# Another order of the query tiles of a head pair, with the turned probabilities kept in other slots by other engines

## The chip, the cores and the metric

One core of one Trainium2 chip runs the whole kernel. The metric is the device time of one execution in microseconds; the median of three executions of the kernel before is 360.82 us.

## The reference, cut to what matters

A decoder layer on x of shape 2 x 512 x 128, in fp32: causal self-attention, a differential cross-attention over a context of 154 rows, and a quantised feed-forward block with a convolution. The change touches the self-attention alone:

```python
q = einsum('ntc,hdc->nhtd', layernorm(x), w_q)        # 16 heads of 64; k and v likewise
a = einsum('nhtd,nhsd->nhts', q, k) / 8
a = where(causal_forbidden, -inf, a)                   # key s > query t is cut
a = softmax(a, axis=3)
y = einsum('nhts,nhsd->nthd', a, v).reshape(n, t, -1) @ w_o
x = x + y
```

## The kernel before

The 16 heads of 2 batch rows are worked off as 16 steps n (`STEPS`), each one pair of heads a = 0, 1 of one batch row. The 512 queries of a pair are four query tiles t = 0 to 3 of 128. Because of the causal mask tile t needs only its first 128(t+1) keys, so tiles 3, 2, 1, 0 are 512, 384, 256 and 128 wide. `ROUNDS` (line 39) packs them in three rounds r: tile 3, tiles 2 and 0 side by side in a bank of 512, tile 1. Round k = 3n + r uses one of two pairs of PSUM banks in turn (`SP[k % 2]`).

A round passes through all engines. TensorE writes the scores (`scores`, matmuls on `qs`, then four small mask matmuls that put -1e30 on what the mask cuts). VectorE takes the row maxima (`row_max`, lines 1122 and 1128). ScalarE takes the exponentials with the row sums (`exps`, line 414; each is followed by a short read of the accumulator). VectorE inverts the sums (`invert_sums`, line 1136) and GpSimd multiplies by them (`normalise`, line 299). TensorE turns the probabilities (`turn`, line 677) in transposes of 64 columns: 16 for a round of 512, 8 for tile 1. Rounds 0 and 1 are turned into the banks PT and PT+1, round 2 into PJ0 and OB. The turned blocks are copied from PSUM to slots of `pT` in SBUF: round 0 half by VectorE (`keep_turned`, line 1150) and half by ScalarE (`keep_half`, line 423), round 1 by VectorE, round 2 by ScalarE (`keep_short`, line 435). Slots 0 and 3 alternate from step to step for tile 3. When all three rounds of a pair are there, TensorE multiplies them with v (`weighted`, ten matmuls per head pair, bank OB), and ScalarE copies the result to `onT` (`copy_heads`, line 445).

Every engine has one queue in order, written out by hand. In step n TensorE does: scores(n,0), turn(n-1,1), scores(n,1), turn(n-1,2), scores(n,2), project(n+1) for keys (bank PJ0) and queries (bank PT), weighted(n-1), turn(n,0). VectorE does: keep_turned(n-1,0), row_max(n,0), keep_turned(n-1,1), invert_sums(n,0), row_max(n,1), row_max(n,2), keys(n+1), invert_sums(n,1), invert_sums(n,2). ScalarE does: copy_heads(n-2), keep_half(n-1), exps(n,0), keep_short(n-1), exps(n,1), query(n+1), exps(n,2). GpSimd normalises rounds 0, 1, 2. Some steps have more behind them: quantise_weights on VectorE after steps 2 and 3, the output projection of the first batch row in step 9, a layer norm on VectorE and ScalarE after step 10 and on VectorE after step 11.

The waits that matter here stand in `scores` and `turn`: scores of round k may start once the exponentials of round k-2 have read their banks, and turn(n,1) may start once the copies of turn(n,0) have emptied the banks PT and PT+1:

```python
if k >= 2:
    pe.wait_ge(exp_done, EXPS[k - 1])     # in scores(n, r), k = 3n + r
...
if r == 1:
    pe.wait_ge(pt_dve, 2 * n + 1)         # in turn(n, r)
    pe.wait_ge(pt_act, 2 * n + 1)
```

After the last step the cross-attention begins: query_parts(0) on ScalarE (its turn stands between exps(15,1) and exps(15,2)), query_rows(0) on VectorE after the last invert_sums, then cross_max(0,0) on TensorE, between whose rounds the last turns and the last weighted sum are placed.

Of the kernel before, what the change touches and what calls it, by code (L numbers as in the profile page):

```python
# [8 lines left out]
ALU = mybir.AluOpType  # L9
# [3 lines left out]
P = 128  # L13
# [25 lines left out]
ROUNDS = [[3], [2, 0], [1]]  # L39
# [18 lines left out]
for _k in range(48):  # L58
    MAXES.append(MAXES[-1] + (2 if _k % 3 == 0 else 1))


PLACE = ({3: 0, 2: 1, 1: 2, 0: 3}, {2: 0, 1: 1, 3: 2, 0: 3})


def decoder_layer(nc, x, consts, wqk, wv, wo, ctxT, xwq, xbq, xwk, xbk, xwv, xbv, xwo, xbo, lam_in,
                  w1, cw, cb, w2, out):
    with ExitStack() as ctx:
# [100 lines left out]
        prob = (pT[:, 4, :, :], pr[:, 0:2, :], pr[:, 2, :].rearrange("p (a n) -> p a n", a=2))  # L168
# [98 lines left out]
        def _(pool):  # L267
# [24 lines left out]
            def normalise(n, r):  # L292
                pool.wait_ge(inv_done, 3 * n + r + 1)
                at = 0
                for t in ROUNDS[r]:
# [70 lines left out]
        def _(act):  # L366
# [38 lines left out]
            def exps(n, r):  # L405
# [4 lines left out]
                for t in ROUNDS[r]:  # L410
                    w = P * (t + 1)
                    for a in range(2):
                        act.wait_ge(max_done, MAXES[k] + 1 + a if r == 0 else MAXES[k + 1])
                        nc.scalar.activation(prob[r][:, a, at:at + w], bank[:, SP[k % 2] + a, at:at + w], ACT.Exp,  # L414
                                             bias=nmax[:, t, a:a + 1], accum_out=psum[:, t, a:a + 1]).then_inc(exp_done, 1)
                    at += w

            def keep_half(n):

                act.wait_ge(t_ps, 3 * n + 1)  # L420
                if n >= 2:
                    act.wait_ge(u_ps, n - 1)
                nc.scalar.copy(turned_to(3 * (n % 2), 2 * NT)[:, 1], turned_from(PT, PT + 2, 2 * NT)[:, 1]).then_inc(
                    pt_act, 1)

            def keep_short(n):

                act.wait_ge(t_ps, 3 * n + 3)
                if n >= 1:
                    act.wait_ge(u_ps, n)  # L430
                for half, at in enumerate((PJ0, OB)):
                    whole = pT[:, 2, :, :]
                    dst = bass.AP(whole.tensor, whole.offset + 64 * half,
                                  [list(whole.ap[0]), [T, 2], [P, 2], [1, 64]])
                    last = nc.scalar.copy(dst, bank[:, at, 0:2 * P].rearrange("p (a i q) -> p a i q", a=2, i=2))
                last.then_inc(pt_act, 1)
# [51 lines left out]
            for n in range(1, STEPS):  # L488
                if n >= 2:
                    copy_heads(n - 2)  # L490
                keep_half(n - 1)
                exps(n, 0)
                keep_short(n - 1)
                exps(n, 1)
                if n + 1 < STEPS:
# [5 lines left out]
                exps(n, 2)  # L501
# [3 lines left out]
            keep_half(STEPS - 1)  # L505
            keep_short(STEPS - 1)
# [95 lines left out]
        def _(pe):  # L602
# [8 lines left out]
            def project(n, w):  # L611
# [7 lines left out]
                if n >= 2 and w == 1:  # L619
                    pe.wait_ge(pt_act, 2 * n - 2)  # L620
# [28 lines left out]
            def turn(n, r):  # L649

                k, blocks = 3 * n + r, (NT, NT, 2)[r]
# [5 lines left out]
                if r == 1:  # L657
                    pe.wait_ge(pt_dve, 2 * n + 1)
                    pe.wait_ge(pt_act, 2 * n + 1)
# [21 lines left out]
            def weighted(n):  # L681

                b, p, odd = n // NPAIR, n % NPAIR, n % 2
                pe.wait_ge(pt_dve, 2 * n + 2)
                pe.wait_ge(pt_act, 2 * n + 2)
                three = slice(odd, odd + 3)
                two = slice(1, 4, 2) if odd else slice(0, 2)
                one = 3 if odd else 0
                for j in range(NT):
                    for a in range(2):  # L690
                        own = slice(DH * a, DH * a + DH)
                        o = bank[own, OB, :].rearrange("p (t q) -> p t q", q=P)
                        v = v_sb[:, b, j, 2 * p + a, :]
                        keys = slice(P * j, P * j + P)
                        if j == 0:
                            mm(o[:, 0:3, :], v, pT[:, three, a, keys], True, False, skip_group_check=True)
                            mm(o[:, 3, :], v, pT[:, 1, a, 3 * P:4 * P], False, False, skip_group_check=True)
                        elif j == 1:
                            mm(o[:, 0:3, :], v, pT[:, three, a, keys], False, False, skip_group_check=True)
                        elif j == 2:  # L700
# [803 lines left out]
```

## Time and profile before

| | |
|---|---|
| median of 3 executions | 360.82 us (359.97 to 361.19) |
| profiled execution, its own time | 358.9 us |
| span of the profiled execution | 356.7 us |
| TensorE busy | 307.7 us, 86% |
| VectorE / ScalarE / GpSimd busy | 226.1 / 212.4 / 121.3 us |
| self-attention, start to last step | about 14 to 198 us of the span |
| mean granted TensorE clock | 0.964 |

Between the first and the last instruction lie 356.7 us; 2.2 us of the profiled execution lie around them. A timeline row has start, duration, engine, line, operation, and in brackets how long the engine idled before it and on whom it waited. PE is TensorE, PEld its weight loads, DVE VectorE, ACT ScalarE, POOL GpSimd.

### The profile page before, as it was taken

The numbers are of one execution on the slowest core, as the hardware profiler recorded it, in microseconds if no ns is written. First come the engines' busy times: TensorE is split into PE (matmuls) and PEld (weight loads), VectorE is DVE, ScalarE is ACT, GpSimd is POOL, SyncE is SP. The second block draws the span as 40 slices with busy tenths as digits, with TensorE's granted clock in tenths as the row PEclk, the third lists the DMA queues.
The fourth block names the chain that finished last, engine by engine and source line by source line (L and its number), as shares of the span: only waits on it lengthen the run. The fifth ranks groups of instructions, "written<-read, shape, count | busy, mean of one in ns | idle before, by whom it ended". The sixth has DMA issues, their size and how long they took to land.

```text
span 356.7 us, 6631 instructions
## 1 busy us (share of the span) xinstructions
PE 307.7 (86%) x2454; PEld 202.4 (57%) x2454; DVE 226.1 (63%) x507; ACT 212.4 (60%) x520; POOL 121.3 (34%) x193
## 2 busy tenths in 40 slices
PE   1797899989999998889997799969999897988795
PEld 0564665666666775656664467735655562465463
DVE  3854667776666527676666564576777768068554
ACT  3465577767777618867774173576786368436154
POOL 4623547774477646625642020113330000000000
PEclk9999899999999999999996889999999999999696
DMA  7800000000000000000000000000000000000001
GB/s 286 299 1 2 0 3 1 2 2 2 3 0 3 2 2 1 2 2 0 2 3 3 0 0 2 0 0 3 0 1 2 0 3 0 0 0 2 0 23 38
DMA packets 4834, 6.17 MB, mean 17 GB/s; under 512 B 833, under 2 KB 3649, under 8 KB 4674
## 3 DMA queue, kind: packets, MB, share of 16 engines
q1 hardware_dynamic: 4514, 5.42, 4.3%
q8 instruction: 19, 0.31, 0.4%
q10 hardware_dynamic: 288, 0.33, 0.3%
q14 instruction: 13, 0.11, 0.1%
HBM read 5.23 MB, written 0.52 MB: 16 GB/s over the span
## 4 chain that ended last, share of the span: by engine, by line
PE 57%; DVE 20%; ACT 14%; issue 6%; POOL 1%; DMA 1%; ACTq 0%; DVEq 0%
PE bank L604 51%; ACT pr L414 4%; ACT pT L414 3%; DVE nmax L1122 3%; DVE nmax L1128 3%; PE bank L677 2%; DVE pT L1150 2%; ACT pT L520 2%; PE bank L805 1%; DVE qk L1179 1%; DVE xn L1072 1%; ACT v_sb L525 1%; DVE onT L1302 1%; DVE stats L1059 1%; POOL pr L299 1%
## 5 line engine op out<-in xcount | busy, mean ns | idle before, releaser
L1179 DVE TENSOR_REDUCE qk<-bank 128x4 fp32r<-128x616 f32 x64 | 49.2, 797 | 24.6 <-PE bank L604 24.3
L520 ACT ACTIVATE pT<-bank 128x512 f32<-128x512 f32 (+1 forms) x80 | 45.0, 600 | 28.4 <-PE bank L604 27.3
L299 POOL TENSOR_SCALAR pr<-pr,pinv 128x384 f32<-128x384 f32 (+2 forms) x96 | 46.3, 505 | 45.1 <-DVE pinv L1136 45.1
L414 ACT ACTIVATE pr<-bank,nmax 128x384 f32<-128x384 f32 (+2 forms) x96 | 44.7, 482 | 18.2 <-DVE nmax L1128 18.2
L604 PE MATMUL bank<-qs 64*128 64x512 f32 (+3 forms) x256 | 49.0, 464 | 4.6 <-ACT pT L414 4.6
L604 PE MATMUL bank<-pT,v_sb 128*64 128x128 f32 (+2 forms) x320 | 39.5, 394 | 0.0
L309 POOL TENSOR_TENSOR km<-kb_,con 128x1232 fp32r<-128x1232 f32 x8 | 18.0, 2248 | 59.4 <-PE bank L604 57.4
L604 PE MATMUL bank<-km,qk 128*128 128x308 f32 x128 | 33.7, 347 | 3.9 <-ACT pr L414 2.0
L1150 DVE COPY pT<-bank 128x512 f32<-128x512 f32 (+1 forms) x32 | 30.4, 951 | 6.8 <-PE bank L677 6.7
L414 ACT ACTIVATE pT<-bank,nmax 128x512 f32<-128x512 f32 x32 | 21.7, 683 | 20.4 <-DVE nmax L1122 20.4
L604 PEld LDWEIGHTS bank<-pT,v_sb 128*64 128x64 f32 x320 | 21.8, 140 | 19.1 <-issue 16.9
L604 PEld LDWEIGHTS bank<-km,qk 128*128 128x128 f32 x128 | 23.8, 197 | 13.5 <-DVE qk L1179 5.0
L604 PE MATMUL bank<-qk,km 128*128 128x512 f32 x64 | 28.5, 451 | 2.3 <-ACT pT L520 2.0
L1128 DVE TENSOR_REDUCE nmax<-bank 128x2 f32<-128x768 f32 (+2 forms) x48 | 29.9, 676 | 0.6 <-PE bank L604 0.6
L299 POOL TENSOR_SCALAR pT<-pT,pinv 128x512 f32<-128x512 f32 x32 | 21.9, 697 | 21.4 <-DVE pinv L1136 21.4
L1136 DVE RECIPROCAL pinv<-psum 128x2 f32<-128x2 f32 x64 | 8.5, 157 | 29.0 <-ACT pr L414 28.1
L604 PEld LDWEIGHTS bank<-qs 64*128 64x128 f32 x256 | 20.2, 188 | 7.5 <-ACT pT L414 6.2
L1122 DVE TENSOR_REDUCE nmax<-bank 128x1 f32<-128x512 f32 x32 | 20.6, 683 | 4.2 <-PE bank L604 4.2
L604 PEld LDWEIGHTS bank<-mask_b,sel_b 64*128 64x128 bf16 x256 | 13.9, 94 | 16.3 <-issue 12.3
L677 PE MATMUL bank<-con,pr 64*128 64x64 f32 x384 | 18.4, 227 | 4.6 <-POOL pr L299 3.0
L414 ACT ACTIVATION_READ_ACCUMULATOR pr<-bank,nmax 128x1 f32 x96 | 20.5, 213 | 0.0
L604 PE MATMUL bank<-qk,wqk_h 128*128 128x512 f32 x48 | 19.2, 444 | 1.4 <-DVE wqk_l L1367 1.4
(162 smaller groups left out, 596.8 us busy)
## 6 DMA issues: line engine op xcount, KB each, us to landing
pT<-in_wqk SPq DMA_DIRECT2D x1, 1024.0 KB, 6.0
cw_sb<-in_cw SPq DMA_DIRECT2D x1, 768.0 KB, 8.9
x_sb<-in_x SPq DMA_DIRECT2D x2, 256.0 KB, 5.2
pT<-in_wv SPq DMA_DIRECT2D x1, 512.0 KB, 6.7
wo_sb<-in_wo SPq DMA_DIRECT2D x1, 512.0 KB, 7.2
out<-x_sb SPq DMA_DIRECT2D x8, 64.0 KB, 1.5
onT<-in_consts ACTq DMA_DIRECT2D x1, 256.0 KB, 6.5
pT<-in_xwk SPq DMA_DIRECT2D x1, 256.0 KB, 7.2
```

Source lines behind the costliest of these rows:

```text
L299: nc.gpsimd.tensor_scalar(d, d, pinv[:, t, a:a + 1], 1.0, ALU.mult, ALU.mult).then_inc(norm_done, 1)
L309: nc.gpsimd.tensor_tensor(km[:, g, :, :], _repeat(kb_[:, g, b, :], GP), _bcast(con[:, C_ROWM:C_ROWM + GP], S2), ALU.mult).then_inc(km_done, 1)
L414: nc.scalar.activation(prob[r][:, a, at:at + w], bank[:, SP[k % 2] + a, at:at + w], ACT.Exp, bias=nmax[:, t, a:a + 1], accum_out=psum[:, t ...
L520: nc.scalar.activation(px[rows, v % 10, :], bank[rows, (ST0, ST1)[v % 2], :], ACT.Exp, scale=SD ** -0.5).then_inc(xexp_done, 1)
L525: nc.scalar.copy(ut[:, G // NG, 2 * (G % NG) + u, :], bank[:, OB, :]).then_inc(ut_done, 1)
L604: return nc.tensor.matmul(out_, lhsT, rhs, start=start, stop=stop, **kw)
L677: last = nc.tensor.transpose(bank[:, to, at:at + 64], prob[r][own, a, P * i:P * i + P], con[own, C_ID + 64 * half:C_ID + 64 * half + 64])
L1122: nc.vector.tensor_reduce(nmax[:, NT - 1, a:a + 1], bank[:, SP[k % 2] + a, :], AX.X, ALU.max, negate=True).then_inc(max_done, 1)
L1128: last = nc.vector.tensor_reduce(nmax[:, t, :], bank[:, SP[k % 2]:SP[k % 2] + 2, at:at + w], AX.X, ALU.max, negate=True)
L1136: last = nc.vector.reciprocal(pinv[:, t, :], psum[:, t, :])
L1150: nc.vector.tensor_copy(dst, src).then_inc(pt_dve, 1)
L1179: nc.vector.tensor_reduce(m, s_in, AX.X, ALU.max, negate=True).then_inc(round_done, 1)
```

## The change

The rounds become tile 1; tile 3; tiles 2 and 0. The order in which each engine takes rounds 0, 1, 2 stays, so what stands in each place is another tile. Turned blocks are laid out by key block and head in turn, in three slots: 0 for tile 3, 1 for tiles 2 and 0, 2 for tile 1; no slot alternates. VectorE copies the turned rounds 0 (tile 1, 512 values per partition) and 1 (tile 3, 1024); ScalarE copies round 2 (tiles 2 and 0, 1024) in two copies of 512, both after exps(n,0) of the next step; keep_half is gone. exps of tile 0 move behind query(n+1). Maxima and inverses of tiles 2 and 0 have semaphore increments of their own. The matmuls of `weighted` are as many and as wide as before, with plain slices.

```diff
-ROUNDS = [[3], [2, 0], [1]]
+ROUNDS = [[1], [3], [2, 0]]
 ...
-    MAXES.append(MAXES[-1] + (2 if _k % 3 == 0 else 1))
-PLACE = ({3: 0, 2: 1, 1: 2, 0: 3}, {2: 0, 1: 1, 3: 2, 0: 3})
+    MAXES.append(MAXES[-1] + (1, 2, 2)[_k % 3])
+PLACE = {3: 0, 2: 1, 1: 2, 0: 3}
+TILES_OF = [sum(len(_r) for _r in ROUNDS[:_k]) for _k in range(4)]
 ...
-        prob = (pT[:, 4, :, :], pr[:, 0:2, :], pr[:, 2, :].rearrange("p (a n) -> p a n", a=2))
+        prob = (pr[:, 2, :].rearrange("p (a n) -> p a n", a=2), pT[:, 4, :, :], pr[:, 0:2, :])
+        turned = pT[:, :, :, :].rearrange("p s a (j q) -> p s (a j) q", q=P)
 ...
             def normalise(n, r):
-                pool.wait_ge(inv_done, 3 * n + r + 1)
                 at = 0
-                for t in ROUNDS[r]:
+                for i, t in enumerate(ROUNDS[r]):
+                    pool.wait_ge(inv_done, NT * n + TILES_OF[r] + i + 1)
 ...
-            def exps(n, r):
+            def exps(n, r, tiles=(0, 1)):
 ...
-                    for a in range(2):
-                        act.wait_ge(max_done, MAXES[k] + 1 + a if r == 0 else MAXES[k + 1])
+                    for a in range(2 if i in tiles else 0):
+                        act.wait_ge(max_done, MAXES[k] + 1 + a if r == 1 else MAXES[k + 1])
 ...
-            def keep_half(n):
-            def keep_short(n):
 ...
+            def keep_last(n, half):
+                if half == 0:
+                    act.wait_ge(t_ps, 3 * n + 3)
+                    if n >= 1:
+                        act.wait_ge(u_ps, n)
+                nc.scalar.copy(turned_to(1, 2 * NT)[:, half], bank[:, (PJ0, OB)[half], :].rearrange(
+                    "p (m q) -> p m q", q=64)).then_inc(pt_act, 1)
 ...
-                keep_half(n - 1)
                 exps(n, 0)
-                keep_short(n - 1)
+                keep_last(n - 1, 0)
+                keep_last(n - 1, 1)
                 exps(n, 1)
+                exps(n, 2, (0,))
                 if n + 1 < STEPS:
                     query(n + 1)
 ...
-                exps(n, 2)
+                exps(n, 2, (1,))
 ...
                 if n >= 2 and w == 1:
-                    pe.wait_ge(pt_act, 2 * n - 2)
+                    pe.wait_ge(pt_act, 2 * n - 3)
 ...
-                k, blocks = 3 * n + r, (NT, NT, 2)[r]
+                k, blocks = 3 * n + r, (2, NT, NT)[r]
 ...
                 if r == 1:
                     pe.wait_ge(pt_dve, 2 * n + 1)
-                    pe.wait_ge(pt_act, 2 * n + 1)
 ...
-                        at = 64 * (blocks * a + i)
+                        at = 64 * (2 * i + a)
 ...
+                        v, tiles = v_sb[:, b, j, 2 * p + a, :], min(3, NT - j)
+                        last = mm(o[:, 0:tiles, :], v, turned[:, 0:tiles, 2 * j + a, :], j == 0, j == NT - 1,
+                                  skip_group_check=True)
                         if j == 0:
+                            mm(o[:, 3, :], v, turned[:, 1, 2 * 3 + a, :], False, False, skip_group_check=True)
 ...
             def invert_sums(n, r):
+                at = EXPS[3 * n + r]
+                for i, t in enumerate(ROUNDS[r]):
+                    dve.wait_ge(exp_done, at + 2 * i + 2)
+                    nc.vector.reciprocal(pinv[:, t, :], psum[:, t, :]).then_inc(inv_done, 1)
 
             def keep_turned(n, r):
                 dve.wait_ge(t_ps, 3 * n + r + 1)
-                if r == 0 and n >= 2:
-                    dve.wait_ge(u_ps, n - 1)
-                if r == 1 and n >= 1:
+                if n >= 1:
                     dve.wait_ge(u_ps, n)
-                slot = 1 if r else 3 * (n % 2)
+                slot, blocks = ((2, 4), (0, 8))[r]
+                nc.vector.tensor_copy(turned_to(slot, blocks), turned_from(PT, PT + 2, blocks)).then_inc(pt_dve, 1)
```

## Rows read from the trace of the kernel before

**Rows 1.** The page: busy time, share of the span, instructions of TensorE.
```profile
PE 307.7 (86%) x2454; PEld 202.4 (57%) x2454; DVE 226.1 (63%) x507; ACT 212.4 (60%) x520; POOL 121.3 (34%) x193
```

**Rows 2.** Waits of TensorE, 92.6 to 110 us (two steps): total, times, longest.
```profile
PE bank L604 <- ACT pT L414: 1.3, 3, 0.6
```

**Rows 3.** Timeline of TensorE, one step: start, duration, operation, idle before.
```profile
102.02 0.50 PE L604 MATMUL bank<-xT_h,wqk_h 128*128 128x512 f32 x1
...
105.93 0.72 PE L677 MATMUL bank<-con,pT 64*128 64x64 f32 x16
106.47 1.09 PE L604 MATMUL bank<-qs 64*128 64x512 f32 x4
...
107.50 0.69 PE L677 MATMUL bank<-con,pr 64*128 64x64 f32 x16
108.00 0.89 PE L604 MATMUL bank<-qs 64*128 64x384 f32 x4
...
109.09 0.30 PE L604 MATMUL bank<-mask_b,sel_b 64*128 64x128 bf16 x4
109.20 0.44 PE L677 MATMUL bank<-con,pr 64*128 64x64 f32 x8
110.00 0.70 PE L604 MATMUL bank<-qs 64*128 64x256 f32 x4 [0.35 <-ACT pT L414]
110.53 0.28 PE L604 MATMUL bank<-mask_b,sel_b 64*128 64x128 bf16 x4
110.74 0.50 PE L604 MATMUL bank<-xT_h,wqk_h 128*128 128x512 f32 x1
```

**Rows 4.** Timeline of VectorE and ScalarE in the same step.
```profile
105.05 0.50 ACT L414 ACTIVATE pr<-bank,nmax 128x256 f32<-128x256 f32 x1
...
105.86 0.24 ACT L414 ACTIVATION_READ_ACCUMULATOR pr<-bank,nmax 128x1 f32 x1
...
106.68 0.69 DVE L1150 COPY pT<-bank 128x512 f32<-128x512 f32 x1 [0.39 <-PE bank L677]
...
107.71 1.29 DVE L1122 TENSOR_REDUCE nmax<-bank 128x1 f32<-128x512 f32 x2 [0.34 <-PE bank L604]
...
108.50 0.69 ACT L414 ACTIVATE pT<-bank,nmax 128x512 f32<-128x512 f32 x1 [1.23 <-DVE nmax L1122]
```

**Rows 5.** Timeline, two disturbed steps: from turn to copy, from copy to turn.
```profile
64.90 0.44 PE L677 MATMUL bank<-con,pr 64*128 64x64 f32 x8
...
65.38 0.65 ACT L435 COPY pT<-bank 128x256 f32<-128x256 f32 x2 [0.16 <-PE bank L677]
...
71.87 0.67 DVE L1150 COPY pT<-bank 128x512 f32<-128x512 f32 x1
...
72.64 0.72 PE L677 MATMUL bank<-con,pr 64*128 64x64 f32 x16 [0.86 <-POOL pr L299]
```

**Rows 6.** The page: the exponentials, tiles 2, 1, 0 and tile 3; busy, mean ns.
```profile
L414 ACT ACTIVATE pr<-bank,nmax 128x384 f32<-128x384 f32 (+2 forms) x96 | 44.7, 482 | 18.2 <-DVE nmax L1128 18.2
L414 ACT ACTIVATE pT<-bank,nmax 128x512 f32<-128x512 f32 x32 | 21.7, 683 | 20.4 <-DVE nmax L1122 20.4
```

**Rows 7.** Timeline of step 11, which follows the layer norm.
```profile
142.32 0.59 ACT L423 COPY pT<-bank 128x512 f32<-128x512 f32 x1
...
143.06 0.71 PE L677 MATMUL bank<-con,pr 64*128 64x64 f32 x16 [1.52 <-ACT pT L423]
...
145.77 0.70 PE L604 MATMUL bank<-qs 64*128 64x256 f32 x4 [0.55 <-ACT pT L414]
```

**Rows 8.** Timeline at the border to the cross-attention.
```profile
183.97 0.58 ACT L414 ACTIVATE pr<-bank,nmax 128x384 f32<-128x384 f32 x1 [1.28 <-DVE nmax L1128]
...
188.92 0.52 PE L604 MATMUL bank<-km,qk 128*128 128x308 f32 x2 [2.05 <-ACT pr L414]
```

**Rows 9.** Windows: length, busy of PE, PEld, DVE, ACT, POOL, granted clock.
```profile
190.00:198.00 8.00, 7.18 (x41) 4.43 (x39) 3.81 (x5) 1.91 (x4) 0.00 (x0) 0.57 0.01 2
```

**Rows 10.** Waits of TensorE, 14 to 43 us: total, times, longest.
```profile
PE bank L604 <- ACT v_sb L461: 2.0, 2, 1.5
```

More of the change, by code:

```diff
@@ L416, in exps @@
                     at += w
-            def keep_half(n):
[L420 to L424, printed above, removed]
-            def keep_short(n):
[L428 to L436, printed above, removed]
+            def keep_last(n, half):
[5 more added lines that the diff above has]
+                    "p (m q) -> p m q", q=64)).then_inc(pt_act, 1)
             def copy_heads(n):
@@ L504, in _ @@
             copy_heads(STEPS - 2)
-            keep_half(STEPS - 1)
-            keep_short(STEPS - 1)
+            keep_last(STEPS - 1, 0)
+            keep_last(STEPS - 1, 1)
             query_parts(1)
@@ L681, in weighted @@
             def weighted(n):
-                b, p, odd = n // NPAIR, n % NPAIR, n % 2
+                b, p = n // NPAIR, n % NPAIR
                 pe.wait_ge(pt_dve, 2 * n + 2)
                 pe.wait_ge(pt_act, 2 * n + 2)
-                three = slice(odd, odd + 3)
-                two = slice(1, 4, 2) if odd else slice(0, 2)
-                one = 3 if odd else 0
                 for j in range(NT):
@@ L692, in weighted @@
                         o = bank[own, OB, :].rearrange("p (t q) -> p t q", q=P)
-                        v = v_sb[:, b, j, 2 * p + a, :]
-                        keys = slice(P * j, P * j + P)
+                        v, tiles = v_sb[:, b, j, 2 * p + a, :], min(3, NT - j)
+                        last = mm(o[:, 0:tiles, :], v, turned[:, 0:tiles, 2 * j + a, :], j == 0, j == NT - 1,
+                                  skip_group_check=True)
                         if j == 0:
[L696 to L700, printed above, removed]
-                            mm(o[:, 0:3:2, :] if odd else o[:, 0:2, :], v, pT[:, two, a, keys], False, False,
-                               skip_group_check=True)
-                        else:
-                            last = mm(o[:, PLACE[odd][3], :], v, pT[:, one, a, keys], False, True, skip_group_check=True)
+                            mm(o[:, 3, :], v, turned[:, 1, 2 * 3 + a, :], False, False, skip_group_check=True)
                 last.then_inc(u_ps, 1)
             def head_tile(b, p, t):
-                at = P * PLACE[(NPAIR * b + p) % 2][t]
+                at = P * PLACE[t]
                 return onT[:, (NPAIR * b + p) % ONT_SLOTS, at:at + P]
@@ L1119, in row_max @@
                 dve.wait_ge(s_ps, k + 1)
-                if r == 0:
+                if r == 1:
                     for a in range(2):
```

15 lines of the change are left out of this document (3 added, 12 removed).

## The prediction

> **What bounds the kernel now.** I read the page first: TensorE is busy for 307.7 of 356.7 us, 86%, and no other engine passes 63% [rows 1]. The self-attention steps are the stage that changes, so I looked there next. The waits of TensorE over two undisturbed steps name one cause only, an exponential of tile 3, 1.3 us in three waits [rows 2]. The timeline of one such step then gives every start [rows 3]. I write S3, S20, S1 for the scores of tile 3, of tiles 2 and 0, and of tile 1; T3, T20, T1 for their turns; P for the projections; W for the weighted sum. Start to start: T3 0.54 (105.93 to 106.47), S3 1.03, T20 0.50, S20 1.20, T1 until S1 0.80, S1 0.74, P and W together 3.91 (102.02 to 105.93). Sum 8.72 us for a step. The one place where TensorE stands still is before S1, at 110.00 [rows 3]. The chain into it is: S3 starts at 106.47, maxima at 107.71, exponentials at 108.50 [rows 4], S1 1.50 us after that, because S1 reuses the banks of S3. Between them TensorE has only S3, T20, S20 and T1 to do.
>
> So at most this stall can go. How large is it start to start? Sixteen transposes are busy 0.72 and take 0.54; eight are busy 0.44 [rows 3]. Eight less cost 0.28 less, so T1 needs 0.26 and the stall is 0.80 - 0.26 = 0.54 us a step.
>
> **The change part by part.** *The same work in another order.* TensorE's matmuls and transposes are as many and as wide as before. A round of tile 1 is now the first, so the wait of the exponentials sits before S20: it reuses the banks of S1. Let S1 start at 0. Masks reach the next instruction in 0.11 us where a turn follows (109.09 to 109.20) and 0.21 where a projection does (110.53 to 110.74) [rows 3]: S1 before T3 needs 0.64, S20 before P needs 1.30.
>
> *The new first wait.* T3 must find PT and PT+1 empty. T1 now stands directly before S1 and fills them, and one copy of 512 by VectorE empties them. A turn of eight is seen by the copying engine 0.48 us after its start (64.90 to 65.38) [rows 5]; S1 starts 0.26 after T1, so the copy starts at 0.22. It takes 0.69 [rows 4], and from the end of such a copy to the turn that waits for it pass 0.10 (72.54 to 72.64) [rows 5]. T3 starts at 1.01 instead of 0.64: a new wait of 0.37 us in every step. Before, S3 with its 1.03 stood in that gap and covered the same copy (106.68 + 0.69 = 107.37 against 107.50) [rows 3, 4]; that cover is gone.
>
> *The old wait.* S3 then starts at 1.01 + 0.52 = 1.53 (a turn of 16 takes 0.50 or 0.54), T20 at 2.56, S20 at 3.07. Are the exponentials of tile 1 done? S1 is complete at about 0.9 and VectorE is through with the copy by then. From maximum to exponential 0.79 (107.71 to 108.50), two exponentials of 256 take 1.05 (105.05 to 106.10) [rows 4], so they end at about 2.75. Slack 0.3: this wait is gone.
>
> *The step.* T1 0.26 + 1.01 + 0.52 + 1.03 + 0.51 + 1.30 + 3.91 = 8.54 us. With 0.50 for both turns it is 8.52; I take that, against 8.72: 0.20 us less a step. The gain is the old stall of 0.54 less the new one of 0.37.
>
> *Copies reassigned.* ScalarE loses keep_half (512) and keep_short (2 x 256), 0.59 [rows 7] and 0.65 [rows 5], and gains two copies of 512, 1.18 at most. Nothing net. But all of it now stands before the exponentials of tile 3. A turn of 16 is seen 0.75 after its start (105.93 to 106.68) [rows 3, 4]: the first copy starts at 2.56 + 0.75 = 3.31 and ends at 3.90; P wants it at 4.37. W wants the second, by 4.5, at 5.96. Both are covered. The two semaphore increments more on VectorE and the dropped alternate slot cost nothing: W(n-1) stands before turn(n,0) in TensorE's queue, so that slot is always read out in time. The Trainium skill (page "VectorE: DVE Perf Modes", section "The DRAIN you can't avoid") says of copies that a semaphore after each costs nothing extra; no row here isolates it.
>
> *The loop through ScalarE.* What could be late next is T20, copies, exponentials of tile 3 and tile 2, query, exponentials of tile 0, inverse, copy of T1, T3, S3, T20 of the next step. By full durations: 0.75 + 2 x 0.59 + 2 x 0.683 + the four exponentials of tiles 2 and 0 (6 x 0.482 - 2 x 0.50 = 1.89) [rows 6, 4] + query 0.60 + last accumulator read and inverse about 0.3 + copy and hand-over 0.79 + 0.52 + 1.03 = 8.43. Successive instructions overlap in part (two exponentials with their reads take 1.05, not 1.24 [rows 4]), so from below it is about 7.9. Against 8.52 it is covered, by 0.1 to 0.6.
>
> *Steps with extra work.* Behind steps 2, 3 and 11 VectorE has work ahead of the copy that T3 waits for. Before, this cost 0.86 at the turn [rows 5] and more in 11. In the new order both the end of the exponentials and the due time of the copy come about 0.3 to 0.4 earlier after the turn: no change, these three steps gain nothing. Step 11 follows the norm of step 10, which holds ScalarE; there TensorE waited 1.52 for keep_half and again 0.55 before S1 [rows 7]. keep_half is gone and the exponentials come a copy earlier (0.59), with the 0.2 of the order somewhat less: 0.7 us less (0.3 to 1.0). The ten other steps from 1 to 14 give 10 x 0.20 = 2.0.
>
> *The border.* cross_max(0,0) waits for ScalarE's last exponentials, 2.05 us [rows 8]. ScalarE itself had waited 1.28 for maxima there [rows 8]; in the new order it waits about 0.55, for T20, in their place (2.75 to 3.31), and it begins 0.6 earlier, measured from turn(14,0), since T1 and S1 are short. Against this its copies are 0.3 longer and the second holds up the projection a little: 0.9 us less (0.4 to 1.3). Behind it turns of 16 instead of 8, and a copy of 1024 instead of 512 before query projection 1, cost 0.3.
>
> *The start.* TensorE waits there twice for value copies that stand behind exponentials, 2.0 us [rows 10]. The first round is shorter, the last is two tiles of exponentials instead of one. The first two waits shrink, and a third arises at the last value tile; I take 0.2 us more (-1 to +1).
>
> *Sum.* -2.0 - 0.7 - 0.9 + 0.3 + 0.2 = -3.1 us. Against the profiled execution, 358.9 us, that is 355.8. The median of the three is 360.82, 0.5% higher; the same -0.86% gives 357.7 us.
>
> **The rivals.** *A, forecast:* 357.7.
>
> *B, the clock stays up at the border.* After the 2.05 us of idling [rows 8] the granted clock of 190 to 198 us was 0.57 in the mean [rows 9], between the levels of 2.4 and 1.2 GHz. At full clock its 7.18 busy us would have taken 0.43 x 7.18 = 3.1 us less at most. The change shortens the idle time there by 0.9. Half of it still stands in the way, and the gaps after it are the same, so I hold it less likely: 357.7 - 3.1 = 354.6. The Trainium skill (page "TensorE: Matmul & The Clock Gate", Part 1) has the clock throttled by default and released by activity, by which a shorter idle time could keep it; the row only shows the fall after the idle time, not what would avoid it.
>
> *C, the gain of the steps is eaten.* If the copy of T1 is seen 0.2 later than by the rows of other places, or the loop through ScalarE comes to 8.7, the step stays at 8.72. What is left is -0.7 - 0.9 + 0.5 = -1.1: 359.7. For it speaks that one slack of 0.1 to 0.6 rests on durations; against it that each hand-over has a row.
>
> *D, slower: the loop through ScalarE binds.* Its place is ScalarE between T20 and the inverse of tile 0, its price every 0.1 us over 8.72 times 14 steps. From 8.72 + (1.1 + 1.1)/14 = 8.88 on the kernel is slower by over 1.1 us, that is 0.45 above the sum of full durations. At 9.0 it gives 360.8 - 1.1 + 14 x 0.28 = 363.6. Against it: that sum is already an upper end, and before, ScalarE waited for maxima (20.4 + 18.2)/16 = 2.4 us a step [rows 6].
>
> *E, the change doesn't do what it says:* the wait for exponentials stays, now before S20, since T3 comes late. It needs maxima 0.3 later than worked out; the step would be 8.6 to 8.7, the time 359 to 359.7, as C.
>
> **How the numbers follow.** A 0.66, B 0.12, C and E 0.14, D 0.08. A's own range, from its terms (step gain 0.1 to 0.3, step 11, border, start), is 355.6 to 359.6. Over all 354.5 to 360.6, which leaves out D and the low end of B. Faster by over 0.3% (a measurement of this kernel can't tell less from no change) means under 359.7: A but for its edge and B, 0.76. Within 0.3%: most of C and E and that edge, 0.16. Slower: 0.08.
>
> **What would show it.** In the trace after: starts of T1 8.5 us apart in undisturbed steps; no wait of TensorE for exponentials of tile 1 (or under 0.1); a wait of 0.3 to 0.4 before T3 for VectorE's copy; first copy by ScalarE 0.75 after the start of T20; cross_max(0,0) about 0.9 earlier after turn(14,0); clock under 1 behind it. Wrong it would be if T1 to T1 is 8.7 or more, if ScalarE's waits are gone, or if the clock falls in another place.

## The result, and the profile after

The changed kernel is slower. Its median is 364.69 us (364.31 to 365.05, four runs) against 360.74 us for the kernel before (359.97 to 361.19, four runs, one more than at the forecast): a ratio of 1.0112, with a 95% interval of 1.0089 to 1.0134. Its profiled execution took 364.31 us with a span of 362.4 us, against 358.9 and 356.7. The forecast was 357.7 us and the range 354.5 to 360.6.

From the page after, busy time and instructions by engine, and the granted clock in 40 slices:

```profile
PE 311.4 (86%) x2454; PEld 205.8 (57%) x2454; DVE 231.2 (64%) x507; ACT 211.8 (58%) x504; POOL 120.5 (33%) x193
...
PEclk9999699999999999699998789999999998999698
```

TensorE has as many instructions as in [rows 1] and the same share of the span, so the page doesn't tell where 5.7 us went. The starts of turn(n,0) do; they stand in both kernels behind the same work. In us:

| stage | before | after | difference | forecast |
|---|---|---|---|---|
| up to turn(0,0) | 42.84 | 44.72 | +1.88 | +0.2 |
| steps 1, 2, 5 to 10, 13, 14 | 95.12 | 94.11 | -1.01 | -2.0 |
| steps 3, 4, 12 | 29.57 | 30.87 | +1.30 | 0 |
| step 11 | 10.62 | 15.03 | +4.41 | -0.7 |
| turn(14,0) to cross_max(0,0) | 10.77 | 10.25 | -0.52 | -0.9 |
| behind it | 167.78 | 167.42 | -0.36 | +0.3 |
| span | 356.70 | 362.40 | +5.70 | -3.1 |

One step holds more than three quarters of the loss. The undisturbed steps do what was said of them, at half the size: eight of the ten in the second row gain 0.09 each. Step 6, where the wait for exponentials had been 0.63 us before, gains 0.36, and step 9, with the output projection in it, loses 0.07.

**An undisturbed step.** Timeline after, TensorE and the engines that feed it, one step of many that are alike:

```profile
107.89 0.46 PE L670 MATMUL bank<-con,pr 64*128 64x64 f32 x8
...
108.18 0.65 PE L598 MATMUL bank<-qs 64*128 64x256 f32 x4
108.39 0.69 DVE L1127 COPY pT<-bank 128x512 f32<-128x512 f32 x1 [0.31 <-PE bank L670]
...
109.23 0.71 PE L670 MATMUL bank<-con,pT 64*128 64x64 f32 x16 [0.28 <-DVE pT L1127]
...
109.75 1.11 PE L598 MATMUL bank<-qs 64*128 64x512 f32 x4
109.77 0.47 ACT L418 ACTIVATE pr<-bank,nmax 128x256 f32<-128x256 f32 x1 [1.19 <-DVE nmax L1111]
...
110.78 0.69 PE L670 MATMUL bank<-con,pr 64*128 64x64 f32 x16
...
111.28 0.89 PE L598 MATMUL bank<-qs 64*128 64x384 f32 x4
...
111.51 1.07 ACT L428 COPY pT<-bank 128x512 f32<-128x512 f32 x2 [0.71 <-PE bank L670]
...
116.51 0.28 PE L670 MATMUL bank<-con,pr 64*128 64x64 f32 x2
```

The reader is to see that S20 at 111.28 follows T20 with no wait: the wait of [rows 2] for exponentials is gone. In its place stands the wait of T3 at 109.23 for VectorE's copy of T1. Start to start: T1 0.29, S1 1.05, T3 0.52, S3 1.03, T20 0.50, then 5.23 until the next T1. The sum is 8.62 us, against 8.72 before. TensorE's waits from 82 to 112 us after (total, times, longest) have this one cause:

```profile
PE bank L670 <- DVE pT L1127: 1.1, 4, 0.3
```

**Step 11.** First the kernel before, VectorE and GpSimd, which extends [rows 7] to the engines that the prediction did not read there:

```profile
141.37 0.34 DVE L1064 TENSOR_SCALAR std<-mv 128x4 f32<-128x4 f32 x1
141.62 0.68 DVE L1150 COPY pT<-bank 128x512 f32<-128x512 f32 x1
141.65 3.45 POOL L350 TENSOR_TENSOR qk<-cw_sb,qk 128x1536 fp32r<-128x1536 f32 x1
```

The same place after:

```profile
141.62 0.46 PE L670 MATMUL bank<-con,pr 64*128 64x64 f32 x8
...
142.62 0.38 DVE L1045 BATCH_NORM_AGGREGATE mv<-stats 128x2 f32<-128x6 f32 x4
143.02 3.42 POOL L354 TENSOR_TENSOR qk<-cw_sb,qk 128x1536 fp32r<-128x1536 f32 x1
143.03 3.43 DVE L1047 TENSOR_SCALAR std<-mv 128x4 f32<-128x4 f32 x1
146.38 0.68 DVE L1127 COPY pT<-bank 128x512 f32<-128x512 f32 x1
...
147.20 1.12 PE L670 MATMUL bank<-con,pT 64*128 64x64 f32 x16 [4.52 <-DVE pT L1127]
...
148.08 2.05 PE L598 MATMUL bank<-qs 64*128 64x512 f32 x4
```

VectorE's operation on four values a partition (std of the layer norm) takes 3.43 us instead of 0.34. It starts 0.01 us behind GpSimd's operation on 1536 values (the low part of the convolution's weights, wc_l from here on) and ends with it. The copy of T1 stands behind it in VectorE's queue, and T3 waits 4.52 us for that copy. Then TensorE runs slow: S3 takes 2.05 us, not the 1.11 of the step above, and the granted clock of this stretch was 0.57 in the mean, between the levels of 1.2 and 2.4 GHz:

```profile
144.00:152.00 8.00, 4.80 (x44) 3.29 (x46) 6.33 (x7) 3.74 (x9) 3.37 (x3) 0.57 0.01 3
```

(Columns as in [rows 9].) In the kernel before, the clock of the same window was 1.00: std had started 0.28 before wc_l, and nothing stood still.

### The profile page after: what moved, and what is told of

It is laid out like the page before. It is cut to its first block, busy times and chain, and to the rows that moved or that the text cites. A ratio compares the mean times of both kernels' runs of the same rounds, so it can differ in the third digit from the quotient of the medians.

```text
span 362.4 us, 6617 instructions
## 1 busy us (share of the span) xinstructions
PE 311.4 (86%) x2454; PEld 205.8 (57%) x2454; DVE 231.2 (64%) x507; ACT 211.8 (58%) x504; POOL 120.5 (33%) x193
## 3 DMA queue, kind: packets, MB, share of 16 engines
HBM read 5.23 MB, written 0.52 MB: 16 GB/s over the span
## 4 chain that ended last, share of the span: by engine, by line
PE 66%; DVE 15%; ACT 9%; issue 7%; DMA 1%; POOL 1%; ACTq 0%; DVEq 0%
PE bank L598 56%; PE bank L670 7%; DVE pT L1127 3%; ACT pr L418 3%; ACT pT L514 2%; DVE qk L1156 2%; PE bank L788 1%; DVE nmax L1111 1%; ACT v_sb L519 1%; DVE onT L1279 1%; DVE stats L1042 1%; DMA x_sb<-in_x 1%; DVE xn L1055 1%; DVE rx L1273 1%; PE bank L709 1%
## 5 line engine op out<-in xcount | busy, mean ns | idle before, releaser
L418 ACT ACTIVATE pr<-bank,nmax 128x256 f32<-128x256 f32 (+2 forms) x96 | 44.7, 475 | 27.9 <-DVE nmax L1111 27.9
L303 POOL TENSOR_SCALAR pr<-pr,pinv 128x256 f32<-128x256 f32 (+2 forms) x96 | 46.0, 496 | 19.8 <-DVE pinv L1119 19.6
L598 PE MATMUL bank<-qs 64*128 64x256 f32 (+3 forms) x256 | 50.1, 471 | 0.0
L1111 DVE TENSOR_REDUCE nmax<-bank 128x2 f32<-128x512 f32 (+2 forms) x48 | 31.5, 685 | 5.3 <-PE bank L598 5.3
L598 PEld LDWEIGHTS bank<-pT,v_sb 128*64 128x64 f32 x320 | 21.5, 139 | 18.9 <-issue 16.6
L598 PE MATMUL bank<-qk,km 128*128 128x512 f32 x64 | 29.3, 463 | 1.7 <-ACT pT L514 1.6
L428 ACT COPY pT<-bank 128x512 f32<-128x512 f32 x32 | 17.2, 589 | 15.0 <-PE bank L670 15.0
L1119 DVE RECIPROCAL pinv<-psum 128x2 f32<-128x2 f32 x64 | 9.7, 159 | 24.0 <-ACT pr L418 23.9
L598 PEld LDWEIGHTS bank<-mask_b,sel_b 64*128 64x128 bf16 x256 | 14.9, 95 | 16.3 <-issue 12.5
L670 PE MATMUL bank<-con,pT 64*128 64x64 f32 x256 | 11.8, 233 | 12.5 <-DVE pT L1127 12.1
L598 PEld LDWEIGHTS bank<-qs 64*128 64x128 f32 x256 | 21.4, 195 | 1.1 <-issue 1.1
```

Of the source, the lines that this page charges most:

```text
L303: nc.gpsimd.tensor_scalar(d, d, pinv[:, t, a:a + 1], 1.0, ALU.mult, ALU.mult).then_inc(norm_done, 1)
L428: nc.scalar.copy(turned_to(1, 2 * NT)[:, half], bank[:, (PJ0, OB)[half], :].rearrange("p (m q) -> p m q", q=64)).then_inc(pt_act, 1)
L598: return nc.tensor.matmul(out_, lhsT, rhs, start=start, stop=stop, **kw)
L670: last = nc.tensor.transpose(bank[:, to, at:at + 64], prob[r][own, a, P * i:P * i + P], con[own, C_ID + 64 * half:C_ID + 64 * half + 64])
L1111: nc.vector.tensor_reduce(nmax[:, t, :], bank[:, SP[k % 2]:SP[k % 2] + 2, at:at + w], AX.X, ALU.max, negate=True).then_inc(max_done, 1)
L1119: nc.vector.reciprocal(pinv[:, t, :], psum[:, t, :]).then_inc(inv_done, 1)
```

## The experiments

Between profiles of kernels with the same code there, the part up to turn(0,0) differs by up to 2.2 us (42.81 in a3, 43.79 in after_again, 45.01 in a2) and the part behind turn(15,0) by up to 1.8 (170.5 before, 172.3 in b1); steps 1 to 15 repeat to some hundredths, but for steps 3 and 4 and the one with the collision. So mechanisms are read from the steps, and totals from medians where there are any. after_again is the changed kernel unaltered, a second time.

> The changed kernel a second time. In its first trace the turns turn(n,0) stand 1.9 us later than before from n = 0 on, and 1.03 us of that is there before the first scores, in a part that the change does not touch; another 4.4 us come in step 11, where a VectorE instruction of 4 values (std) took 3.43 us while GpSimd's 3.42 us subtraction wc_l, begun 0.01 us before it, was running. Theory P (VectorE stands still until GpSimd's instruction is over, and the new order brings the two together): std over 3 us again, step 11 near 15 us, kernel 364 to 365 us. Theory N (a hiccup of that one execution): std 0.2 to 0.4 us, step 11 near 10.5 us, and the time below 362 us. The 1.03 us at the start: it varies from execution to execution if it is the phase of the clock (low until 19 us there, until 16 us before), and comes again if it is the kernel.

Measured: 364.91 us, ratio 1.0156 [1.0105, 1.0207] to the kernel before on the same chip. The collision is there again: wc_l at 143.91 for 3.42 us, std at 143.92 for 3.44, T3 late by 4.53, step 11 15.69 us. So it isn't a chance of one execution: in both profiles GpSimd is first by 0.01 us. Step 3 is 11.79 here, not 10.20. In both executions T3 waits 1.85 us there, but here the granted clock falls behind it (0.68 in the mean over 64 to 68 us), and T20 takes 1.13 us and S20's scores of tile 2 1.66, not 0.69 and 0.89. Step 4 is 10.06, not 9.84: VectorE's first operation of the quantisation, on 128x512, takes 0.90 us at 72.96, beside GpSimd's normalising, where it took 0.47 at 72.28 in the first profile. That looks like the same hold on a smaller scale; no run isolates it.

**wc_l two steps later, in the new order (a1_wc_later).**

```
-                if n == 10:
+                if n == 12:
                     pool.wait_ge(wcs, 1)
                     nc.gpsimd.tensor_tensor(wc_l, wc[:, :, :], wc_h.bitcast(F32), ALU.subtract).then_inc(wcs, 1)
```

> The changed kernel with GpSimd's subtraction wc_l two steps later, after step 12 instead of after step 10, where VectorE has no norm to do. Theory P: std falls to 0.2 to 0.4 us, the wait of T3 in step 11 from 4.5 to 1.4 us, the low clock behind it is gone, step 11 is 10.3 to 10.8 us instead of 15.0, and the kernel is 4 to 4.7 us faster than the changed one: 360 to 360.7 us, a ratio to before of 0.998 to 1.0. Rival (the norm is late in the new order for another reason, for instance ScalarE's root): step 11 stays over 13 us and the ratio at 1.01.

Measured: 361.13 us, ratio 1.0035 [1.0003, 1.0068]. Timeline of step 11:

```profile
143.31 0.17 DVE L1047 TENSOR_SCALAR std<-mv 128x4 f32<-128x4 f32 x1
143.38 0.69 DVE L1127 COPY pT<-bank 128x512 f32<-128x512 f32 x1
...
144.22 0.71 PE L670 MATMUL bank<-con,pT 64*128 64x64 f32 x16 [1.27 <-DVE pT L1127]
...
147.12 0.92 PE L598 MATMUL bank<-qs 64*128 64x384 f32 x4 [0.65 <-ACT pr L418]
```

std takes 0.17, step 11 falls from 15.03 to 10.49, and no other step moves by more than 0.02. The median falls by 3.8 us against after_again, a little less than the 4 to 4.7 expected, and the ratio stays above 1.0. One line of GpSimd's queue, which the change does not touch, was what made the changed kernel 1.1% to 1.6% slower instead of about 0.3%.

**The same move in the old order (b1_wc_later).**

> The kernel before with the same move of wc_l. In its trace the two instructions miss each other by 0.28 us (std 141.37 to 141.71, wc_l from 141.65). Theory P: nothing changes, step 11 stays at 10.6 us, ratio 0.998 to 1.002. If the move gave the kernel before something too (0.5 us or more), it would be worth something by itself and a1 would say less about the collision.

Measured: 360.2 us, ratio 1.0013 [0.9983, 1.0043]; step 11 10.63. Moving wc_l is worth nothing where it doesn't collide. So the gain of a1 is not that of a better place for wc_l as such.

**The collision made on purpose in the old order (b2_three_stats).** Three bn_stats of 128 columns are repeated ahead of the norm's statistics (they write the same values once more), so that std comes behind wc_l.

```
                 if n == 10:
+                    for t in range(3):
+                        link(nc.vector.bn_stats(stats[:, t, :], x_sb[:, t, :]))
+                    settle()
                     norm_stats(0)
```

> The kernel before with three bn_stats more (each computed twice) ahead of the norm after step 10, about 0.7 us of VectorE work, so that std begins after wc_l has begun. Theory P: std takes 2.5 to 3.2 us, step 11 grows by 3 us and more with the low clock behind it, ratio 1.008 to 1.014, and the kernel before is then as slow as the changed one. Rival (no exclusion, only 0.7 us of extra work): step 11 grows by 0.7 us, ratio 1.001 to 1.003.

Measured: 364.12 us, ratio 1.0135 [1.0089, 1.0181]; step 11 15.56 instead of 10.63, of which step 12 gives back 0.7 (9.61 instead of 10.32). Timeline:

```profile
141.24 3.43 POOL L350 TENSOR_TENSOR qk<-cw_sb,qk 128x1536 fp32r<-128x1536 f32 x1
141.27 0.38 DVE L1062 BATCH_NORM_AGGREGATE mv<-stats 128x2 f32<-128x6 f32 x4
141.68 3.00 DVE L1064 TENSOR_SCALAR std<-mv 128x4 f32<-128x4 f32 x1
144.60 0.68 DVE L1150 COPY pT<-bank 128x512 f32<-128x512 f32 x1
```

std starts 0.44 behind wc_l and again ends with it, after 3.00. The aggregate at 141.27 runs its usual 0.38 beside wc_l, so it is not VectorE as a whole that is held, but this kind of operation. The old order gets slower by 3.9 us (364.12 against 360.22), about as much as the changed kernel is. Not all of it is the collision: the three repeated statistics take 0.66 us themselves, and no run has them without it. But std alone lasts 2.7 us longer, and the clock falls behind it as in the changed kernel (0.57 over 144 to 152 us). So the collision is no property of the new order, only a matter of who starts first.

**VectorE's side work out of the way (a2_extras_moved).** On top of a1, the side work of VectorE (quantising, norm statistics, applying the norm) goes ahead of the last inversion of sums, into the time in which VectorE waits for it.

```
                 invert_sums(n, 1)
-                invert_sums(n, 2)
                 if n in (2, 3):
                     quantise_weights(n - 2)
                 if n == 10:
                     norm_stats(0)
                 if n == 11:
                     norm_apply(0, 3)
+                invert_sums(n, 2)
```

> a1 with VectorE's extra work (quantise_weights, norm_stats, norm_apply) before invert_sums(n,2) instead of behind it, where VectorE idles for about 2 us a step. Theory Q: in the new order every such microsecond lies on the way to the copy that T3 waits for, without the old stall to take it up. Steps 3, 4 and 12 fall from 10.20, 9.84, 10.83 to 8.6 to 8.8, 8.6 to 8.8 and 9.3 to 9.6; step 11 falls by 0.3 to 1.0, since ScalarE's root and its two table loads stay. In all 4 to 5 us. Rival (the inverses of tiles 2 and 0 come too late, and T20 waits for them): the steps fall by less than half of that.

Measured once: 357.12 us, span 355.0. Steps 3, 4, 11 and 12 went from 10.20, 9.84, 10.49 and 10.83 in a1 to 8.63, 8.63, 9.64 and 9.67, together 4.8 us less; the others stayed. What it removes is seen in the changed kernel's step 3:

```profile
62.27 0.71 DVE L1074 TENSOR_SCALAR onT<-w_sb,wscale 128x512 f32<-128x512 f32 x1
...
63.01 0.47 DVE L1076 TENSOR_SCALAR onT<-onT 128x512 f32<-128x512 f32 x1
63.52 0.49 DVE L1079 TENSOR_SCALAR w_sb<-onT,wmean 128x512 f32<-128x512 f32 x1
...
64.04 0.69 DVE L1127 COPY pT<-bank 128x512 f32<-128x512 f32 x1
...
64.88 0.72 PE L670 MATMUL bank<-con,pT 64*128 64x64 f32 x16 [1.85 <-DVE pT L1127]
```

Three operations of the quantisation stand between turn(2,0), at 61.97, and the copy of it. T3 waits 1.85 for the copy, and its own 0.28 is part of that.

**The same move in the old order (b3_extras_moved)**, with the move of wc_l as well.

> The order before with wc_l after step 12 and VectorE's extra work ahead of invert_sums(n,2), without the edit at the start. It says what that work costs in the old order, where the stall before S1 takes up a part: steps 3, 4 and 12 from 9.78, 9.46, 10.32 to 8.7, 8.7, 9.4, in all 2.5 to 3.5 us, against the 4.8 us that the same edit gave in the new order.

Measured once: 356.53 us, span 354.2. Steps 3, 4, 11 and 12 went from 9.78, 9.46, 10.63 and 10.32 in b1 to 8.76, 8.72, 10.11 and 9.62: 3.0 us less. So side work on VectorE cost the old order 3.0 us and the new one 4.8. In steps 3, 4 and 12 alone it is 2.5 and 3.9, and without it these steps are 0.15 shorter in the new order (26.93 against 27.10): this is what the 1.30 us of steps 3, 4 and 12 is made of.

**The copy of T1 halved (a3_split_first).** On top of a1, ScalarE copies the second half of the first turn while VectorE copies the first; T3 waits for both.

```
+            def keep_first(n):
+                act.wait_ge(t_ps, 3 * n + 1)
+                if n >= 1:
+                    act.wait_ge(u_ps, n)
+                nc.scalar.copy(turned_to(2, 4)[:, 1], turned_from(PT, PT + 2, 4)[:, 1]).then_inc(pt_first, 1)
...
+                keep_first(n - 1)
                 exps(n, 0)
```

> a1 with the copy of the turned tile 1 halved: VectorE copies one bank (256 values per partition), ScalarE the other, behind copy_heads. Theory W: T3's wait for that copy is what is left of the stall in each step. The copies end at T1 + 0.9 to 1.0 instead of 1.2, T3's wait falls to 0 to 0.1 us, undisturbed steps from 8.63 to 8.34 to 8.40 us, and the wait of S20 for exponentials stays away, with 0.2 us of slack. 12 to 14 steps give 3.0 to 4.0 us. Rival (the loop through ScalarE is just as long, and its copy comes on top of it): steps stay at 8.55 to 8.75 us.

Measured once: 355.12 us, span 353.3. Timeline:

```profile
87.54 0.46 PE L681 MATMUL bank<-con,pr 64*128 64x64 f32 x8
...
87.84 0.65 PE L608 MATMUL bank<-qs 64*128 64x256 f32 x4
...
88.05 0.42 DVE L1141 COPY pT<-bank 128x256 f32<-128x256 f32 x1 [0.31 <-PE bank L681]
88.13 0.38 ACT L428 COPY pT<-bank 128x256 f32<-128x256 f32 x1
...
88.66 0.71 PE L681 MATMUL bank<-con,pT 64*128 64x64 f32 x16
```

No wait is listed before T3 any more, and undisturbed steps take 8.40 instead of 8.63. The idle time was 0.28; 0.23 of it comes back at each step. T3 still follows the copies, though: it starts 0.15 after the end of ScalarE's (88.51), the same as behind VectorE's copy before this edit (109.08 to 109.23). From S1 to T3 it is 0.82 from start to start, against 1.05 in the changed kernel and the 0.64 that the prediction has for S1 alone. By that estimate 0.18 of the wait is left, too little idle time for the profile to list. No other wait of TensorE is listed for 82 to 112 us. Steps 1 to 15 together take 140.1 us against 143.5 in a1; the other part of the 5.8 us of span lies in the start (42.81 against 44.98), which this edit doesn't touch.

**Value copies ahead of the last exponentials (a5_value_first).** On top of a1, ScalarE makes the copy of value tile 6 before the two tiles of exponentials of the last round, not after them.

```
-            exps(0, 2)
             value_copy(6)
+            exps(0, 2)
             value_copy(7)
```

> a1 with the value copy 6 ahead of exps(0,2) on ScalarE. In three traces of the new order the clock is at half for 5 to 7 us from 34 to 36 us on and turn(0,0) comes 8.4 to 8.7 us after the first stacked keys; in three of the old order it is 6.93 (no fall of the clock, two traces) or 7.92 (a fall). Theory S: the new last round of two tiles puts a wait of 1.5 us (instead of none) right before the wait for the value copies, and TensorE idles 2.5 us within 3.5. Without the first of them the wait of 1.53 us at 34 us goes, the stretch from the first scores to the first stacked keys falls from 16.1 to 14.9 to 15.4 us, and the clock stays up or falls for a shorter time: stacked keys to turn(0,0) 6.9 to 8.0 us. Rival (the fall of the clock has nothing to do with that wait): 8.4 to 8.7 us again.

Measured once: 360.86 us, span 359.0; turn(0,0) at 42.52 instead of 44.98. First the changed kernel, then a5, TensorE where the value projections end and the context's keys begin:

```profile
33.99 0.50 PE L598 MATMUL bank<-km,xT_h 128*128 128x512 f32 x1 [1.53 <-ACT v_sb L454]
...
36.11 1.88 PE L598 MATMUL bank<-km 128*128 128x308 f32 x6 [1.16 <-DVE v_sb L1173]
38.23 1.95 PE L598 MATMUL bank<-km 128*128 128x308 f32 x6 [0.25 <-ACT onT L406]
```

```profile
33.31 0.40 PE L598 MATMUL bank<-km,xT_h 128*128 128x512 f32 x1
34.69 1.08 PE L598 MATMUL bank<-km 128*128 128x308 f32 x6 [0.99 <-ACT v_sb L454]
36.36 1.95 PE L598 MATMUL bank<-km 128*128 128x308 f32 x6 [0.59 <-ACT onT L406]
```

In the changed kernel two waits, 1.53 and 1.16, end within 2.1 us of each other, and the first six matmuls behind them take 1.88 us instead of 1.08. In a5 the first wait is gone, and from the first scores to the context's keys it takes 14.28 us instead of 16.10 in a1, less than the 14.9 to 15.4 expected. That is 1.8 us, and it comes from the edit. The granted clock of 34 to 42 us, mean: 0.62 after, 0.79 in a5, 0.79 before, 1.00 in b1. That the clock stays up longer in a5 because of the edit is not shown: a3, which has a1's code there and both waits (1.53 and 0.98), was at 0.79 too and took 7.79 us from the keys to turn(0,0), where a5 took 7.84 and a1 8.66. In the profile of a5 step 3 was 11.79 instead of 10.20, as in after_again and again at a lower clock, so its one time shows less than the start gained.

**The four edits together in the new order (best_new_order), and the three that the old order can have (best_old_order).** The first has wc_l later, the side work ahead, value copy 6 first and the halved copy. The second has wc_l later, the side work ahead and value copy 4 before its round's exponentials; its copy of a turn is covered by S3 and needs no halving.

> The new order with all four edits: wc_l after step 12, VectorE's extra work ahead of invert_sums(n,2), the copy of turned tile 1 halved between VectorE and ScalarE, value copy 6 ahead of exps(0,2). If the causes are apart from each other they add up: undisturbed steps 8.40 us, steps 3 and 4 too, 12 near 9.4, step 11 9.4 to 9.7, start 14.3 us from first scores to first stacked keys. Against a1 (359.1 us of span) that is 14 x 0.2 + 5 + 1.8 = 9.6 us, with a part lost to the clock: 350 to 353 us, ratio to before 0.970 to 0.982. If they share a cause, the ratio is 0.983 or more.

> The order before with the same care: wc_l after step 12, VectorE's extra work ahead of invert_sums(n,2), and value copy 4 ahead of exps(0,1), where that order has its wait of 1.54 us. Undisturbed steps stay at 8.72 us, with the stall before S1. Steps 3, 4, 12 fall to 8.7, 8.7, 9.4, step 11 by up to 0.5 us, the start by 1.5 us: about 4.5 us, ratio 0.984 to 0.992. If the new order is worth something once its own traps are gone, best_new_order is 0.5 to 1.5% faster than this; if the order as such is worth nothing, the two are within 0.3%.

Measured, medians of six: best_new_order 347.78 us, ratio 0.9666 [0.9624, 0.9707] to the kernel before; best_old_order 354.8 us, ratio 0.9844 [0.9802, 0.9885]. The first is faster than its expectation (0.970 to 0.982), the second lies at the edge of its own. Their ratio, 0.9666 / 0.9844 = 0.982, is what the new order together with the halved copy is worth once its traps are gone: 1.8%, beside the same edits elsewhere, and more than the 0.5 to 1.5% expected.

It is not the order alone. Steps 1 to 15 take 135.9 us in the one profile and 140.4 in the other, 4.5 less. Without the halved copy, a2 against b3, they take 138.7 and 140.4: 1.7 less for the order, the other 2.8 for the halving. The starts up to turn(0,0) are alike (40.96 and 40.58). Behind turn(15,0) the one profile is 4.3 us shorter (168.2 against 172.5) at a higher granted clock (0.95 against 0.92 in the mean), and that part differs by 1.8 between kernels with the same code; how much of it the order brings is open.

Undisturbed steps take 8.40 and 8.71. The page of best_new_order:

```profile
PE 304.4 (88%) x2454; PEld 200.3 (58%) x2454; DVE 225.8 (65%) x507; ACT 216.4 (63%) x520; POOL 120.9 (35%) x193
```

One more edit has no time: the exponentials of tile 2 waiting for tile 2's maximum alone (a6_own_maximum), with 0.2 to 0.3 us less expected in each of steps 3, 4 and 12. ScalarE and VectorE would then read one PSUM bank with nothing that orders them, so it was left out, and what it would bring is open.

## Why the prediction was wrong, step by step

**What bounds the kernel: right.** The stall before S1 was the one wait of the step, and it is gone. No wait of TensorE for exponentials is left in 82 to 112 us.

**The step: right in mechanism, mis-sized by half.** Forecast 8.52, measured 8.62 or 8.63. The wait of T3 was forecast as the new one. Term by term: T1 until S1 0.29 (forecast 0.26); S1 until T3 1.05 (1.01); turn of 16 0.52 and 0.50 (0.50 each); S3 1.03 (1.03); the rest from S20 to the next T1 5.23 (1.30 + 3.91 = 5.21). So 0.03, 0.04, 0.02 and 0.02: each hand-over a little longer than its row, and taking 0.50 where the rows gave 0.50 or 0.54 rounded it further down (the text has the gain as 8.72 less 8.52, 0.20, and as 0.54 less 0.37, 0.17). Against a gain of 0.20 these hundredths are half. The hand-over from copy to turn is 0.15 (109.08 to 109.23), where the prediction took 0.10 from a turn that [rows 5] put down to GpSimd and not to the copy. The copy of T1 is seen 0.50 after T1's start (107.89 to 108.39), where the row of ScalarE gave 0.48. The cost of this term over ten steps is 1.0 us of the 8.8 between the forecast difference (-3.1) and the measured one (+5.7). The term that a3 later cut by 0.23, the wait of T3, stood in the prediction as 0.37 from start to start (1.01 - 0.64) and measured 0.41 (1.05 - 0.64), of which the profile lists 0.28 as idle: it was known, and what wasn't asked is whether another engine could take half of that copy.

**"Steps with extra work", step 11: the step that failed.** The text gave -0.7 and it was +4.41; this alone turns the sign. The part that it looked at did happen: keep_half is gone, and with wc_l out of the way step 11 takes 10.49, less than the 10.62 before, though 0.13 less and not 0.7. Even there the term was too large: it took the wait for ScalarE's copies away and put nothing in its place, but the norm's statistics on VectorE stand before the copy of T1 and before the maxima of S1. In a1 T3 waits 1.27 for that copy, where the turn had waited 1.52 for keep_half, and S20 waits 0.65 for exponentials, where S1 had waited 0.55.

What it did not look at is VectorE and GpSimd beside each other. Measured from turn(10,0), wc_l came 1.86 us later before and 1.40 after. In both GpSimd normalises without a pause until then; this run of work began 0.88 before the turn and took 2.78 before, and began 1.75 before it and took 3.19 after. std came 1.58 later before and 1.41 after. The order of two instructions that no line of the diff names turned round by 0.01 us. The kernel before showed the danger: std ended at 141.71, wc_l had begun at 141.65, and an instruction of 3.45 us stood next to one of 0.34 that the path needs. The runs after_again, a1, b1 and b2 show it in both directions: 15.03 and 15.69 with the collision in the new order and 10.49 without, 15.56 with it in the old order and 10.63 without.

The Trainium skill (page "SBUF — State Buffer", section "Who interferes with whom") states this rule, and the prediction didn't weigh it: VectorE's second pair of SBUF ports is GpSimd's only one, whoever starts first holds it for its whole instruction, and the other stands still, if it is of a kind that needs that pair; it names tensor_scalar among those that can, and says that the order of issue decides. The trace agrees: 3.43 and 3.00 against 0.34 for the tensor_scalar. Of the aggregate, which ran its 0.38 beside wc_l, the section says nothing by name; it isn't held.

**"Steps with extra work", steps 3, 4 and 12: wrong in the step "no change".** It said that the end of the exponentials and the due time of the copy move earlier alike. But before, S3 stood between the copy behind the side work and the turn that waits for it, and the stall before S1 took up some lateness too; after, T3 waits for that copy directly, and every 0.1 us arrives at TensorE. b1 to b3 against a1 to a2 show it: the same side work costs 3.0 us in the old order and 4.8 in the new one. The end of ScalarE's chain, behind which the side work begins, came late too: the sum for it let the exponentials of tile 2 follow those of tile 3 at once, but they wait for the maxima of both tiles, and S20, now last, delivers these late. Later in the step shown above:

```profile
112.71 1.29 DVE L1111 TENSOR_REDUCE nmax<-bank 128x2 f32<-128x768 f32 x2 [0.25 <-PE bank L598]
...
114.09 0.58 ACT L418 ACTIVATE pr<-bank,nmax 128x384 f32<-128x384 f32 x1 [0.16 <-DVE nmax L1111]
```

The wait of 0.16 says that ScalarE had nothing left to do before it. The step before ends alike: ScalarE's last read ends at 107.88 (107.66 + 0.22), VectorE's inverse at 108.08, and the copy of T1 starts at 108.39. Those 0.3 us are all the room for side work, where three operations of the quantisation need 1.7. The loop through ScalarE (rival D) thus keeps 0.3 of slack in an undisturbed step and never bound it; a3 ran it at 8.40.

**The start: wrong in size.** +1.88 against +0.2, forecast with a spread of 1. 1.03 of it lies before the first scores (19.86 against 18.83), where both kernels run the same code. It goes with the moment at which TensorE gets faster: matmuls on 128x512 take 0.63 us until about 18.8 us after and about 16.6 before, and 0.40 behind that. The two clock levels would do this, but the profile's windows give 1.00 on both sides, so it isn't shown. The first scores stand at 18.92 to 20.41 in six profiles of the new order and at 18.83 to 19.79 in four of the old. So it isn't of the change.

From the first scores to the context's keys after took 16.25 us and before 16.09, and the other profiles with this code 16.09 to 16.11: the third wait ("a third arises at the last value tile") came, and the sum of the waits stayed the same. From the keys to turn(0,0) it took 8.61 against 7.92, at a granted clock of 0.62 against 0.79 in the mean of 34 to 42 us. This effect, the clock, the prediction didn't count. Five profiles of the new order without a5's edit took 8.62, 8.40, 8.66, 8.62 and 7.79 there, four of the old 7.92, 6.93, 6.94 and 8.04; that leans to the change as the cause, and no experiment shows it. When the clock falls there stays open: it fell in before and b3 and not in b1 and b2, which have the same code in that stretch.

**The border: right in mechanism, half the size.** -0.52 against -0.9. ScalarE waited 0.71 for T20 and 0.16 for maxima, 0.87 where 0.55 was forecast. TensorE's wait there is 1.82, against the 2.05 of [rows 8]:

```profile
194.98 0.53 PE L598 MATMUL bank<-km,qk 128*128 128x308 f32 x2 [1.82 <-ACT pr L418]
```

Rival B, the clock that stays up, did not come: cross_max(0,0) stands 6 us later than before, and the fall that [rows 9] show behind it comes here too, in 198 to 202 us (last number but two):

```profile
194.00:198.00 4.00, 2.84 (x34) 2.20 (x36) 3.84 (x6) 0.51 (x2) 1.22 (x4) 0.79 0.00 0
198.00:202.00 4.00, 3.71 (x17) 2.45 (x15) 1.42 (x3) 1.89 (x4) 0.00 (x0) 0.50 0.02 4
```

**The rivals and the range.** C, a gain eaten within the step, came half true. D was the only case on the slower side and had the wrong place. The case that happened, another engine's long instruction in front of VectorE, was no rival at all, and so the range ended 4 us under the result. It could have been found by asking of each moved wait who stands in the queue ahead of the one waited for, and what each of these needs that another engine may hold.

## What to carry to other kernels

When a change makes the path wait for an engine that it did not wait for before, list what stands in that engine's queue ahead of the awaited instruction in every disturbed step, with its duration at its worst and not at its mean. Where a long GpSimd instruction and a short VectorE one start within a few tenths of each other, treat their order as undecided and price both; b1 shows that taking the long one away costs nothing, and b2 what a collision can cost (3.9 us, with 0.66 of repeated statistics in it). A reordering that loses can still be the better one: measure it again with its traps removed, as best_new_order against best_old_order does, and keep apart what the order brings and what comes from an edit that only one of the two can use.

## What the runs showed of the hardware

- A tensor_scalar on 128x4 values took 3.43, 3.44 and 3.00 us beside a GpSimd tensor_tensor on 128x1536, and 0.17 to 0.34 without it. It ended when GpSimd ended. A batch-norm aggregate (0.38) and VectorE's copy from PSUM (0.68 at 141.62 before, with GpSimd busy from 141.65 to 145.10) took what they take elsewhere.
- One wait of TensorE of 4.52 us was followed by a granted clock of 0.57 in the mean over 144 to 152 us, and S3 took 2.05 us instead of 1.11. So a blocked instruction of 3.4 us cost 4.5 us of the step: 15.03 against 10.49.
- After a wait of TensorE of 1.85 us in step 3 the granted clock stayed at 1.00 in after (65 to 70 us) and in a1, and fell in after_again and a5 (0.66 in the mean over 64 to 69 and 63 to 68 us): the step took 10.20 us or 11.79, with the same code in that stretch.
- Halving a copy of 512 between two engines took it from 0.69 to 0.42 and 0.38 us, not to half: the listed wait of 0.28 is gone, and it brought 0.23 a step.
